# Layer 3 of a gated cross-attention stack: expert sums take turns with the next stream's opening steps, and a first program in another order

## What is computed

```python
x = x + tanh(g_ffn[2])   * L2_ffn(layernorm(x), ...)      # 8 experts, silu(up) * gate, down
x = x + tanh(g_xattn[3]) * L3_xattn(layernorm(x), ctx, ...)
x = x + tanh(g_ffn[3])   * L3_ffn(layernorm(x), ...)
# L3_xattn
x1_rep = relu(einsum('bld,hd->blh', x1, W))
x2_rep = relu(einsum('bld,hd->blh', x2, W))
scores = einsum('bih,bjh->bij', x1_rep * diagonal, x2_rep)
alpha  = softmax(scores + m[:, None, :], axis=-1)
return einsum('bij,bjd->bid', alpha, x2)
# L3_ffn
router_weights = softmax(einsum('bsd,ed->bse', x, W_router) + b_router, axis=-1)   # all but the two largest set to 0
expert_out = einsum('bsd,eod->bseo', x, W_experts) + b_experts
return einsum('bseo,bse->bso', expert_out, router_weights)
```

## Time and profile before

| | us |
|---|---|
| median of 3 runs | 1021.7 (1021.55 to 1022.72) |
| the profiled execution | 1020.5 |
| its span, first to last instruction | 1018.7 |
| TensorE busy | 882.3 (87%) |
| VectorE busy | 685.1 (67%) |
| ScalarE busy | 470.4 (46%) |
| GpSimd busy | 119.3 (12%) |
| mean granted TensorE clock | 0.97 of full |

### The profile page before, as it was taken

How to read it: one execution, slowest core, us unless ns; L and a number is a source line. 1 busy time by engine, 2 the same in 40 slices (tenths; PEclk the granted TensorE clock), 3 DMA queues, 4 the chain that set the end, 5 groups by cost and what they waited for, 6 DMA issues and landing times.

```text
span 1018.7 us, 14302 instructions
## 1 busy us (share of the span) xinstructions
PE 882.3 (87%) x4731; PEld 598.6 (59%) x4731; DVE 685.1 (67%) x2069; ACT 470.4 (46%) x1134; POOL 119.3 (12%) x206
## 2 busy tenths in 40 slices
PE   2698999968778689789999999999999988899966
PEld 1355545433435566666667676767666766677744
DVE  3845726392866967967668678768766777877734
ACT  0376565677586565565353442443253232322312
POOL 3000100040221301300001001001000111100112
PEclk9999999988899999989999999999999999999989
DMA  6800000000000000000000000000000000000000
GB/s 174 249 1 2 1 1 1 1 0 1 1 1 1 1 1 1 1 2 1 1 1 2 1 1 1 1 1 2 1 1 1 1 1 11 1 11 1 2 10 11
DMA packets 12063, 12.70 MB, mean 12 GB/s; under 512 B 3758, under 2 KB 7896, under 8 KB 11992
## 3 DMA queue, kind: packets, MB, share of 16 engines
q1 hardware_dynamic: 9272, 9.98, 3.2%
q10 hardware_dynamic: 2336, 1.29, 0.5%
q0 software_dynamic: 384, 0.53, 0.2%
HBM read 10.75 MB, written 1.05 MB: 12 GB/s over the span
## 4 chain that ended last, share of the span: by engine, by line
PE 59%; DVE 24%; ACT 7%; issue 5%; POOL 2%; ACTq 0%; POOLq 0%; DVEq 0%
PE bank L1680 10%; PE bank L1668 6%; PE bank L1588 5%; PE bank L1670 5%; PE bank L1669 5%; DVE nm L1188 3%; PE bank L1473 3%; PE bank L1601 3%; DVE hb L1332 3%; DVE hb L1323 2%; DVE x L1312 2%; PE bank L1726 2%; PE bank L1426 2%; PE bank L1651 2%; PE bank L1645 2%
## 5 line engine op out<-in xcount | busy, mean ns | idle before, releaser
L1000 ACT ACTIVATE hb<-bank 96x512 f32<-96x512 f32 (+1 forms) x160 | 95.1, 594 | 203.1 <-PE bank L1670 202.5
L1680 PEld LDWEIGHTS bank<-m_w,hb 128*128 128x128 f32 (+1 forms) x1280 | 166.1, 195 | 23.1 <-issue 5.5
L1668 PE MATMUL bank<-parts,m_w_lo 128*96 128x512 f32 (+1 forms) x320 | 152.1, 475 | 31.4 <-DVE hb L1323 22.7
L1680 PE MATMUL bank<-m_w,hb 128*128 128x128 f32 (+1 forms) x1280 | 175.6, 281 | 2.3 <-DVE hb L1323 2.1
L1332 DVE SCALAR_TENSOR_TENSOR hb<-hb,bank 96x512 f32<-96x512 f32 (+1 forms) x160 | 109.1, 682 | 96.2 <-ACT hb L1000 95.4
L1670 PE MATMUL bank<-parts,m_w_hi 128*96 128x512 f32 (+1 forms) x320 | 127.3, 398 | 0.0
L1669 PE MATMUL bank<-parts,m_w_hi 128*96 128x512 f32 (+1 forms) x320 | 127.1, 397 | 0.0
L1323 DVE TENSOR_TENSOR hb<-hb,bank 96x512 f32<-96x512 f32 (+1 forms) x160 | 109.8, 686 | 10.5 <-PE bank L1670 5.0
L1668 PEld LDWEIGHTS bank<-parts,m_w_lo 128*96 128x96 f32 (+1 forms) x320 | 59.0, 184 | 78.9 <-DVE hb L1323 34.6
L1601 PE MATMUL bank<-Qs,KT 112*77 112x512 f32 x192 | 88.7, 501 | 2.7 <-DVE invt L1238 1.4
L1485 PE MATMUL bank<-KT,Qs 96*128 96x308 f32 x192 | 77.2, 424 | 13.2 <-ACT PTs L909 7.1
(11 more groups left out here) (271 smaller groups left out, 1482.0 us busy)
## 6 DMA issues: line engine op xcount, KB each, us to landing
m_w_raw<-in_L_ffn_w_dram SPq DMA_DIRECT2D x2, 1024.0 KB, 6.6
m_w<-in_L_ffn_W_dram SPq DMA_DIRECT2D x1, 1408.0 KB, 9.5
x<-in_x_dram ACTq DMA_DIRECT2D x4, 256.0 KB, 6.6
out_dram<-x SPq DMA_DIRECT2D x4, 256.0 KB, 2.0
f_out<-in_L_ffn_Wout_dram POOLq DMA_DIRECT2D x8, 64.0 KB, 3.3
m_w_raw<-in_L_ffn_W_experts_dram SPq DMA_DIRECT2D x1, 512.0 KB, 10.5
ctxn<-in_ctx_dram ACTq DMA_DIRECT2D x4, 38.5 KB
Wq<-in_L_xattn_Wq_dram SPq DMA_DIRECT2D x2, 64.0 KB
```

Of the source, the lines that this page charges most:

```text
L1000: act.activation(hb[n % 3][0:m, :], bank[UP[u, n]][0:m, :], ACT.Tanh, scale=0.5).then_inc(*chunk_act.up(u, n))
L1668: pe.matmul(dst, w_lo, x_hi, start=True, stop=False)
L1680: op = pe.matmul(bank[7][:, t * P:(t + 1) * P], hb[n % 3][0:m, t * P:(t + 1) * P], wd, start=i == 0 and t == 0, stop=ends_expert(k, n) and ...
```

## The change

**First program.** On VectorE the scaling of `f0_out` and the whole mask block move ahead of the wait for "small"; then come the six widenings, `bo`, `f0_in`, and last `f0_bias` and `t_w1b`. On TensorE the three matmuls for `bo` wait for "small" only and signal by themselves; those for `t_w1b` follow; `f0_wout`'s, which alone needs "side", is last.

**Gates.** `pre` of F3 has 9 steps. The gates are turned in the body at tile 2, into bank 2, ScalarE copies them there, and the bias matmuls and their addition move from tile 2 to tile 4. VectorE waits for the finished gates at the head of the body.

**Turns.** For A13 and A17 (`TWINS`), each of the first four body steps is followed by one of the first four steps of the next unit's `pre` (A14, A18): statistics, nothing, normalization, transposes. The context's projection for x2 (L1527) moves from step 3 to 4. The body of A17 is no longer beside F11 but behind it (`mine[:-later]`, `"A" * later`).

```diff
-                for i in range(len(groups)):
-                    dve.wait_ge(*kept(i))
-                dve.wait_ge(*landed["small"].at("all"))
...
+                dve.wait_ge(*kept(2))
                 dve.wait_ge(*landed["f0"].at("all"))
                 for c in range(C0):
                     dve.tensor_scalar(f0_out[:, c, :], f0_out[:, c, :], f0_cols[:, 2, c:c + 1], None, ALU.mult)
...
                 dve.wait_ge(*landed["rows"].at("all"))
...
+                for i in range(len(groups)):
+                    dve.wait_ge(*kept(i))
+                dve.wait_ge(*landed["small"].at("all"))
...
+                dve.wait_ge(*turned.at("bo"))
...
-                for name in ("small", "side"):
-                    pe.wait_ge(*landed[name].at("all"))
-                pe.matmul(bank[0][:, 0:1], f0_wout[:], f0_b2[:], start=True, stop=True)
+                pe.wait_ge(*landed["small"].at("all"))
                 for l in range(3):
-                    pe.matmul(bank[2][0:2, l * P:(l + 1) * P], bv[:, l:l + 1].to_broadcast([P, 2]), Wo[l][:], start=True, stop=True)
+                    op = pe.matmul(bank[2][0:2, l * P:(l + 1) * P], bv[:, l:l + 1].to_broadcast([P, 2]), Wo[l][:], start=True, stop=True)
+                op.then_inc(*turned.up("bo"))
...
+                pe.wait_ge(*landed["side"].at("all"))
+                pe.matmul(bank[0][:, 0:1], f0_wout[:], f0_b2[:], start=True, stop=True).then_inc(*turned.up("columns"))
...
+    TWINS, EARLY3 = (13, 17), 4
...
-        return {"F0": 5, "A3": 12}.get(k, 11)
+        return {"F0": 5, "A3": 12, "F3": 9}.get(k, 11)
...
-        return [1.0] * (steps_pre(k) + steps_body(k))
+        early, shared = (EARLY3 if u[1] - 1 in TWINS else 0), (EARLY3 if u[1] in TWINS else 0)
+        return [1.0] * (steps_pre(k) - early + steps_body(k) + shared)
...
-            yield from merged([w for j in beside[i] for w in weights_a(("A", j))], weights_f(("F", i)))
+            mine = [w for j in beside[i] for w in weights_a(("A", j))]
+            if i + 1 == ATTENTIONS:
+                later = len(mine) - len(weights_a(("A", 16))) - steps_pre("F3")
+                mine = mine[:-later]
+            yield from merged(mine, weights_f(("F", i)))
+        yield from "A" * later
...
-                yield from chain(ahead, body(("A", i)))
+                yield from ahead
                 ahead = pre(("A", i + 1))
+                for at, _ in enumerate(body(("A", i))):
+                    yield
+                    if i in TWINS and at < EARLY3:
+                        next(ahead)
+                        yield
...
-                        if i == 10 and k == "F3":
-                            act.wait_ge(*xf_low.at(u))
-                            act.wait_ge(*gates_turned.at(u))
-                            act.activation(gT, bank[2][0:E, :], ACT.Copy).then_inc(*gates_ready.up(u))
...
+                        if n == 2:
+                            act.wait_ge(*xf_low.at(u))
+                            act.wait_ge(*gates_turned.at(u))
+                            act.activation(gT, bank[2][0:MOE3, :], ACT.Copy).then_inc(*gates_ready.up(u))
...
+                    dve.wait_ge(*logits_vector.at(u, "whole"))
...
-                        if n == 2:
-                            dve.wait_ge(*x_done.at(u, 0, E3 - 1))
+                        if n == 4:
+                            dve.wait_ge(*x_done.at(u, 0, "rest"))
                             dve.wait_ge(*ffn_psum.at(u, "bias"))
...
                         if n == 2:
+                            free(2)
+                            pe.wait_ge(*logits_vector.at(u, "whole"))
+                            for i in range(T):
+                                op = pe.transpose(bank[2][0:MOE3, i * P:(i + 1) * P], gw[s][:, i, 0:MOE3], ident[:])
+                            op.then_inc(*gates_turned.up(u))
+                            reader[2] = (gates_ready, u)
+                        if n == 4:
                             pe.wait_ge(*gates_ready.at(u))
```

More of the change, by code:

```diff
@@ L484, in _ @@
                     pe.wait_ge(*kept(i))
[L485 to L487 removed]
+                pe.wait_ge(*landed["small"].at("all"))
                 for l in range(3):
[L489 removed]
+                    op = pe.matmul(bank[2][0:2, l * P:(l + 1) * P], bv[:, l:l + 1].to_broadcast([P, 2]), Wo[l][:], start=True, stop=True)
+                op.then_inc(*turned.up("bo"))
                 for f in range(3):
[L491 to L492 removed]
+                    pe.matmul(bank[1][:, f * 64:(f + 1) * 64], ident[0:3, f:f + 1].to_broadcast([3, P]), t_w1T[:], start=True, stop=True)
+                pe.wait_ge(*landed["side"].at("all"))
+                pe.matmul(bank[0][:, 0:1], f0_wout[:], f0_b2[:], start=True, stop=True).then_inc(*turned.up("columns"))
         main(nc, a, out, dict(locals()))
@@ L1524, in pre @@
                         transpose_x()
-                        if k == "A3":
+                    elif k == "A3":
+                        if i == 4:
                             free(1)
@@ L1528, in pre @@
                             reader[1] = (x2_relu, u)
-                    elif k == "A3":
                         if i == 5:
@@ L1567, in pre @@
                             reader[c] = (logits_vector, u, "logits")
-                        if i == 9 and k == "F3":
-                            free(c)
-                            pe.wait_ge(*logits_vector.at(u, "whole"))
-                            for t in range(T):
-                                op = pe.transpose(bank[c][0:E, t * P:(t + 1) * P], gw[s][:, t, 0:E], ident[:])
-                            op.then_inc(*gates_turned.up(u))
-                            reader[c] = (gates_ready, u)
                     yield
```

38 lines of the change are left out of this document (18 added, 20 removed).

## The result

The changed kernel takes 1027.6 us (median of 5 runs, 1026.4 to 1029.9), the kernel before 1021.7 us. The ratio is 1.0058 with a 95% interval of 1.0043 to 1.0073, so the change makes the kernel 0.6% slower. 1015.2 was forecast, and the range ended at 1019.0.

What follows compares the result with a forecast made beforehand. TensorE, busy 87% of the span, was taken as the bound, with waits at the opening and the end. Opening -5.0, F11 with hand-over +0.6, last sum -2.1, F10 0: -6.5, so 1020.5 - 6.5 + 1.2 = 1015.2 us, range 1011.0 to 1019.0.

Steps and rivals of the forecast that it cites:

- F10, value 0 with 1.5 either way: Layer-3 exchange for stream 0 beside F10: nothing leaves it, net 0, range -1.5 to +1.5 us.
- The opening, -5.0: First program: VectorE finishes at 24.5 instead of 29.57 us, so the next program starts 5.0 us earlier.
- the landing of "rows": First program: the loads the mask block waits for, last issued at 14.45, were taken to land at 17.5 us.
- The bound of 20.5: First program: late limit for "rows", from the 6.1 us that "small" needed; the gain would be 2.0 us.
- rival (b): First program: "rows" lands at 20.5, total 1018.2 us; chance 0.10.
- F11 shrinks by 8.0: F11 stage: with A17's body gone from beside it, the last matmul ends about 8.0 us sooner.
- Rival (d): F11 without cover is bound by its chain, 79.2 us for 24 chunks; total 1023.8 us, slower; chance 0.04.
- The hand-over, +8.6 at low clock: After F11's last matmul: A17's body with stream 3's opening costs 6.6 us more, plus 2.0 at low clock.
- Rival (a): Hand-over after F11 runs at full clock, total 1013.2 us; chance 0.22.
- (c): F11 shrinks by 5 instead of 8 us, total 1018.2 us; chance 0.12.
- (e): The change does more than it says: F10 also wins 1.5 or more, total 1013.5 us; chance 0.07.
- The last sum, -2.1: Stream 3's expert sum: first addition follows the gates at once, last tiles start at 1009.55 instead of 1011.69, -2.1 us.

Runs made afterwards that it cites:

- e5: e4 with the expert sum's opening kept at 11 steps, the last two empty: 1018.2 us, ratio 0.9955.
- e10: e4 with each of the nine opening steps weighing 11/9 in the merging rule, same instructions: 1015.4 us, ratio 0.9938.
- e8: Kernel before with the new first program, the ten "rows" loads issued behind the first stream's x and ctx: 1016.2 us, ratio 0.9938.
- e2: Changed kernel with the first program of before: 1029.1 us, ratio 1.0067.
- e9: Changed kernel with the expert sum's opening put back to 11 steps, the last two empty: 1023.8 us, ratio 1.0015.
- e13: Changed kernel with each of the nine opening steps weighing 11/9 in the merging rule: 1020.1 us, ratio 0.9988.
- e14: e13 without turns, A17's body still behind F11: 1020.1 us, ratio 0.9985.
- e6: e5 with A17's turns and its body behind F11: 1021.6 us, ratio 0.9994.
- e4: Changed kernel without turns and with A17's body beside F11 as before: 1028.3 us, ratio 1.0067.
- e7: e6 with 16 filler matmuls ahead of the transposes of A18 and of A19: 1018.7 us, ratio 0.9966.

## Why the prediction was wrong, step by step

**F10, value 0 with 1.5 either way: the step that failed.** It measured +6.7. I counted the instructions that the change moves in layer 3 and found nothing added. What I did not count is that two steps fewer in each opening move the other steps of A12 to A15 against F10's, since `merged` spreads the steps by their weights; the shares of 0.629, 0.635 and 0.636 above could have been worked out from the code. I also excused VectorE's queue with "VectorE is busy without a gap there". That was the reason to look closer: it stands between two tracks, so whatever comes one place later waits for a whole router chain. The lower bound took the wait that goes, 2.17 us, as its measure, the upper one the row sums behind `rstd`; neither allowed for a reduction that falls behind another unit's chain. 4.0 us at one place and half speed behind it was outside of that. e5 and e10 show the cause: with `nm` ahead of the chain again, F10 takes 104.8 and 100.6 us.

**The opening, -5.0.** It measured -2.2 at the first statistics. The failing term is the landing of "rows", taken at 17.5; VectorE's wait for it ended at 19.99. The bound of 20.5 (six us from its issue) was nearly met, and with it the sum says -2.0, rival (b). The rest of the chain held to the tenth: masks 1.67 us, then 5.3 us without a pause (21.66 to 26.92). e8 shows that the gain is real when rows comes earlier, -6.8 at the first statistics and -6.1 in the total. In the profile of after the lead of 2.2 is gone by 315 us, where the code is unchanged but the low-clock stretches lie elsewhere. I take this for scatter between executions: e8 kept its lead to the end on average, and e2, whose code up to F10 is that of before, starts F10 at 791.0 us, where before starts it at 788.6.

**F11 shrinks by 8.0.** It shrank by 10.4 in after, by 5.8 to 7.2 in e9, e13 and e14 (78.3 to 72.0, 72.5 and 71.1). Between kernels that differ in the body's place alone, it is 7.2 both times (e5 to e6, e10 to e13). The work that leaves is 7.7 us (72.69 - 65.00 busy at the same clock; I had 7.1). How much idle time goes with it depends again on where the steps fall: 3.0 us are left in after, 5.3 in e13 (before 5.6), where a low stretch (911.5 to 915.5) also lengthens the busy time (67.2 against 65.0). Rival (d), a bare chain of 79 us, is refuted: 24 chunks took 68.0.

**The hand-over, +8.6 at low clock.** It measured +9.5. Here the working held. These are rows of after, TensorE, then VectorE, then GpSimd:

```profile
975.50 1.16 PE L1455 MATMUL bank<-ident,xna 128*128 128x128 f32 x4 [3.46 <-DVE xna L1106]
976.58 2.07 PE L1735 MATMUL bank<-m_b,xfa 8*128 8x128 f32 x8
```

```profile
974.09 0.80 DVE L1358 TENSOR_TENSOR x<-PTs,x 128x128 f32<-128x128 f32 x1 [1.20 <-POOL PTs L836]
974.81 1.31 DVE L1106 TENSOR_SCALAR xna<-x,mv_a,rstd_a 128x128 f32<-128x128 f32 x4
```

```profile
971.79 1.04 POOL L808 TENSOR_TENSOR rstd_a<-rstd_a,minus_half 128x4 f32<-128x4 f32 x1
972.80 0.72 POOL L834 TENSOR_TENSOR PTs<-PTs 128x256 f32<-128x256 f32 x1
```

F11's last matmul ends at 967.75. The row sum behind `rstd` releases the addition 6.3 us later (forecast 6.6), the normalizations start at 7.1 (6.9), TensorE idles 3.46 us (3.0) and then runs at 1.2 GHz: transposes 1.16 (1.15), bias 2.07 (2.2). The score matmuls come 21.0 us behind (20.1), before 11.5. (The three clock terms of the prediction add up to 2.35, not 2.0.) The hand-over was well sized. Net of F11 and hand-over the change gives -0.9, where +0.6 was forecast, but that this comes so near is partly luck: with the steps back in place the same two stages cost 3.0 us more than without moving the body (e5 to e6: 101.6 to 104.6) and 2.8 more (e10 to e13: 102.2 to 105.0). Rival (a), full clock, is refuted. So are (c), F11 shrinking by 5 only, and (e), a gain in F10. But the reason given for (a), that 3.0 us is below every idle time after which the clock fell, was wrong already in before: an idle time of 2.10 us ends at 789.05 there, and this is the clock behind it:

```profile
789.70:793.00 3.30, 3.30 (x14) 2.99 (x14) 1.63 (x4) 0.72 (x2) 0.00 (x0) 0.54 0.00 0
```

The length of the idle time alone doesn't decide. I took the right level from a comparison of lengths that doesn't bear it.

**The last sum, -2.1.** It measured -0.4 in after, -1.9 to -2.2 in e4, e5 and e10, and -1.9 in e9. The order of events is the one forecast, and the size is right where the clock recovers in time. In after it doesn't:

```profile
996.00:1010.00 14.00, 9.33 (x37) 6.59 (x38) 6.89 (x41) 1.46 (x3) 1.27 (x2) 0.51 0.00 0
```

In before the stretch at 1.2 GHz ran from 991 to 998.5, and the router's matmuls stand at its end:

```profile
998.27 1.06 PE L1564 MATMUL bank<-m_router,xfa 128*128 128x8 f32 x8
```

In after it begins in the idle time of 4.85 us ahead of the transposes at 1000.67. TensorE, then VectorE:

```profile
1004.37 1.88 PE L1579 MATMUL bank<-m_router,xfa 128*128 128x8 f32 x8
1006.10 3.24 PE L1412 MATMUL bank<-mask_q,identb 128*128 128x308 bf16 x12
1008.95 0.82 PE L1741 MATMUL bank<-m_w_hi,Qs 128*128 128x512 f32 x1
```

```profile
1008.02 0.68 DVE L1284 TENSOR_TENSOR Qs<-xfa,Qs 128x512 fp32r<-128x512 f32 x1
...
1009.54 0.19 DVE L1160 TENSOR_TENSOR gw<-gw,gs 128x32 f32<-128x32 f32 x1
1010.49 1.51 DVE L1373 SCALAR_TENSOR_TENSOR x<-bank,gw,x 128x128 f32<-128x128 f32 x4 [0.76 <-PE bank L1741]
```

The router's matmuls take 1.88 us, and the gates are ready 9.55 us behind the start of the normalization instead of 8.68: 0.87 lost. Tile 0 needs the low part of x, which is ready at 1008.70, so the fillers ahead of it held it by 0.25 us at most; its matmuls then start at half speed. The first addition, which should follow the gates at once, comes 0.76 us behind them, where it was 2.00: 1.24 won. From there to the end both kernels take 11.4 us. 0.87 - 1.24 is the -0.4. I had weighed the clock for the hand-over only, and not for what follows it.

**The sum.** Forecast -5.0 + 0.6 - 2.1 + 0 = -6.5. Measured to the end: -2.2 opening, +2.4 on the way to F10 (scatter), +6.7 F10, -0.9 F11 with the hand-over, -0.4, in sum +5.6. The chance of slower was 0.04, all of it on a rival that was not the cause.

## What to carry to other kernels

Where a rule merges two tracks by steps or weights, taking empty steps out is a change of the whole schedule. Diff the order of each in-order engine around its longest chains, not only the edited place, and try the same instructions at two or three phases (here 1028.3 and 1015.4 us). Price a wait of TensorE with what comes behind it: with 10 to 14 us more of F10 at half clock the same 514 matmuls took 4.7 to 6.6 us more, and a few cheap matmuls in the waits of the last two stages gave part of such a loss back in e7. And look at what stands ahead of a small load in its queue before you reorder those who wait for it.
